# Last cross attention of a decoder kernel: the turn and the projections take other places among the scores, pair 16 is weighed in its own PSUM bank, and GpSimd's last sums wait for a scaling

## What is computed

```python
# self attention: 16 heads of 64, then out projection and residual
z = softmax(q @ k.T / 8) @ v;   x = layernorm(x + (x + z @ w_o))
# cross attention: 2 heads of 64; keys are 154 of the context and the 512 of x itself
ln = layernorm(x) * g + b
q  = ln @ Wq.T
kv = concat([xn_ctx @ Wkv.T, ln @ Wlkv.T]);  k, v = split(kv)
q  = rmsnorm(q, qn_g) / 8;   k = rmsnorm(k, kn_g)
out = softmax(mask(q @ k.T)) @ v @ Wo.T + bo
x  = layernorm(x + out)
```

## Time and profile before

| | |
|---|---|
| median of 3 runs | 696.09 us (694.47 to 698.51) |
| the profiled execution's own time | 697.45 us |
| its span in the profile | 695.7 us |
| PE busy | 617.9 us (89% of the span) |
| DVE busy | 451.1 us (65%) |
| ACT busy | 287.3 us (41%) |
| POOL busy | 246.7 us (35%) |
| mean granted clock of TensorE | 0.951 of full |

### The profile page before, as it was taken

One profiled execution on the slowest core, in us unless ns is written; L12 is line 12 of the kernel. 1 busy time (PEld: TensorE's weight loads), 2 busy tenths in 40 slices (PEclk: granted clock), 3 DMA queues, 4 the chain that ended last, 5 costly groups with the idle time before them and its releaser, 6 DMA issues.

```text
span 695.7 us, 8771 instructions
## 1 busy us (share of the span) xinstructions
PE 617.9 (89%) x3161; PEld 307.6 (44%) x3162; DVE 451.1 (65%) x1172; ACT 287.3 (41%) x548; POOL 246.7 (35%) x178
## 2 busy tenths in 40 slices
PE   8766769998997899999999979997878999999996
PEld 4322457976752322222224422333522446565655
DVE  6999998457679457666765597687626673333234
ACT  7979966032403564444443344341141342212120
POOL 2897443233501554554464444572150100000001
PEclk9957979999998999999999999998997999999999
DMA  8200032030000000000000000001400000000000
GB/s 316 93 0 0 2 121 124 1 122 1 1 1 0 0 1 0 1 0 1 2 0 1 1 0 1 0 1 63 195 0 1 1 1 1 0 1 0 1 1 31
DMA packets 3681, 18.92 MB, mean 27 GB/s; under 512 B 917, under 2 KB 2198, under 8 KB 3126
## 3 DMA queue, kind: packets, MB, share of 16 engines
q1 hardware_dynamic: 3638, 18.36, 6.9%
HBM read 17.84 MB, written 0.52 MB: 26 GB/s over the span
## 4 chain that ended last, share of the span: by engine, by line
PE 62%; DVE 20%; ACT 9%; issue 5%; POOL 4%; POOLq 0%; DVEq 0%; ACTq 0%
PE PS L2339 10%; PE PS L1617 8%; PE PS L2353 6%; DVE SB L1846 6%; PE PS L1562 4%; PE PS L1601 4%; PE PS L1585 3%; PE PS L1687 2%; PE PS L1631 2%; PE PS L2063 2%; DVE SB L199 2%; PE PS L2074 1%; DVE SB L1868 1%; ACT SB L468 1%; POOL SB L238 1%
## 5 line engine op out<-in xcount | busy, mean ns | idle before, releaser
L1832 POOL TENSOR_TENSOR SB<-SB 128x1024 f32<-128x1024 f32 x32 | 75.3, 2353 | 115.3 <-ACT SB L1785 115.3
L1846 DVE TENSOR_REDUCE SB<-PS 128x2 f32<-128x1024 f32 x64 | 78.4, 1225 | 56.7 <-PE PS L1585 56.7
L1785 ACT ACTIVATE SB<-PS 128x1024 f32<-128x1024 f32 x64 | 65.5, 1023 | 101.3 <-PE PS L1604 101.2
L2339 PE MATMUL PS<-SB 128*128 128x512 f32 x176 | 83.1, 609 | 0.2 <-DVE SB L2416 0.2
L1617 PE MATMUL PS<-SB 128*64 128x512 f32 x256 | 69.9, 628 | 1.4 <-DVE SB L1871 1.4
L1601 PE MATMUL PS<-SB 64*128 64x512 f32 x256 | 68.9, 616 | 1.1 <-ACT SB L1789 1.1
L238 POOL TENSOR_TENSOR SB<-SB 128x4 f32<-128x4 f32 x18 | 19.4, 1078 | 133.0 <-DVE SB L204 132.9
L2391 ACT ACTIVATE SB<-PS 128x512 f32<-128x512 f32 (+1 forms) x48 | 28.5, 596 | 90.2 <-PE PS L2339 87.3
L2416 DVE TENSOR_TENSOR SB<-SB,PS 128x512 f32<-128x512 f32 (+1 forms) x48 | 32.6, 686 | 48.1 <-PE PS L2339 43.7
L2353 PEld LDWEIGHTS PS<-SB 128*128 128x128 f32 (+1 forms) x384 | 49.4, 190 | 18.5 <-issue 10.0
L1868 DVE RECIPROCAL SB<-PS 128x512 f32<-128x512 f32 x16 | 53.7, 3355 | 3.9 <-PE PS L1631 3.9
(11 more groups left out here) (401 smaller groups left out, 1132.8 us busy)
## 6 DMA issues: line engine op xcount, KB each, us to landing
SB<-exp SPq DMA_DIRECT2D x1, 4352.0 KB, 14.0
SB<-moe SPq DMA_DIRECT2D x1, 4096.0 KB, 12.3
SB<-dft SPq DMA_DIRECT2D x1, 2304.0 KB, 12.1
SB<-att SPq DMA_DIRECT2D x1, 2048.0 KB, 8.1
SB<-mix SPq DMA_DIRECT2D x1, 768.5 KB, 4.5
SB<-mix SPq DMA_DIRECT2D x1, 640.0 KB, 5.6
SB<-ssm SPq DMA_DIRECT2D x1, 602.0 KB, 6.7
SB<-lat SPq DMA_DIRECT2D x1, 585.0 KB
```

The costliest lines, as they stand in the source:

```text
L1785: act.activation(expd[i % 2][:, 1024 * u:1024 * u + 1024], bank(2 * (u % 2), 2), ACT.Exp).then_inc(sem("d_exp"), 1)
L1832: pool.tensor_tensor(half_sums[half], e[:, 0:1024], e[:, 1024:], ALU.add).then_inc(sem("d_half_sum"), 1)
L1846: dve.tensor_reduce(shift[i % 2][:, qt:qt + DK + 1:DK], two_heads(bank(4, 2)), AX_X, ALU.max, negate=True)\
L2339: pe.matmul(bank(2 * (i % 3) + side), exp_w["e_w13"][:, c:c + 128], xsT[:, 512 * n:512 * n + 512], start=True, stop=True).then_inc(sem(("t ...
```

## The change

Five things, no instruction more or less:

- The weighing of pair 16 goes to bank 0 instead of bank 6 (`heads_bank`), and no longer waits for `d_headed` of pair 15. The out projection of the second batch goes to bank 6 in turn. All four of its steps stand together, with the turn of the context keys and of row tiles 0 and 1 ahead of them, in that order.
- POOL waits for `e_scaled` 3, the scaling of row tiles 2 and 3 on DVE, before the half sums and the sum of pair 16.
- `e_maxima` and the parts of the out projection of batch 2 interleave in another way; the fourth `e_maxima` comes behind the out projection of pair 16, and on DVE its maximum behind the residual and the statistics of the norm.
- In the cross attention the turn of batch 1's normed rows comes ahead of all scores, the projections 4 to 7 come between the first two scores, and the turns of tiles 2 and 3 and the four `e_maxima` of batch 1 come among the scores and weighings of batch 0.
- `shifts(1)` comes ahead of `sums(0)`, and DVE's last sum of batch 0 (`late_sum`, L2264) between its maxima of batch 1.

```diff
     def weigh(i, kt):
             if kt == 0:
                 pe.wait_ge(sem("d_exp"), 4 * i + 4)
-                if i >= 1:
+                if 1 <= i < NP_ - 1:
                     pe.wait_ge(sem("d_headed"), i)
...
-                ins = pe.matmul(bank(6)[head(h), :], v, expd[i % 2][...],
+                ins = pe.matmul(heads_bank(i)[head(h), :], v, expd[i % 2][...],
...
         e_turn_ctx(pe)
-        weigh(last, 0)
-        weigh(last, 1)
+        e_turn_tiles(pe, 0)
+        e_turn_tiles(pe, 1)
+        for kt in range(4):
+            weigh(last, kt)
         e_maxima(pe, 0, 0)
-        weigh(last, 2)
-        weigh(last, 3)
+        pe.wait_ge(sem("d_headed"), last)
+        pe.matmul(bank(6), zeros_low, mask_16[0:1, 0:512], start=True, stop=False)
+        attended_part((0,))
         e_maxima(pe, 0, 1)
         sums(last)
-        pe.matmul(bank(0), zeros_low, mask_16[0:1, 0:512], start=True, stop=False)
-        attended_part((0, 1))
+        attended_part((1, 2))
         e_maxima(pe, 0, 2)
-        attended_part((2, 3))
-        e_maxima(pe, 0, 3)
+        attended_part((3,))
         pe.wait_ge(sem("d_headed"), NP_)
...
         ins.then_inc(sem("d_out"), 1)
+        e_maxima(pe, 0, 3)
...
     def d_pool(pool):
             if i == NP_ - 1:
                 for k in range(3):
                     e_pool_row_norms(pool, k)
+                pool.wait_ge(sem("e_scaled"), 3)
...
     def e_pe(pe):
         shifts(0)
+        turn_half(pe, tiled(xn), "e_normed", 1, 1, 5)
         score(0, 0)
-        for u in range(KT):
...
+        e_project(pe, 4)
+        e_project(pe, 5)
+        score(0, 1)
+        e_project(pe, 6)
+        e_project(pe, 7)
+        weigh(0, 0)
+        score(0, 2)
+        weigh(0, 1)
+        score(0, 3)
         e_turn_tiles(pe, 2)
+        weigh(0, 2)
         e_turn_tiles(pe, 3)
-        for qt in range(4):
-            e_maxima(pe, 1, qt)
+        score(0, 4)
+        weigh(0, 3)
+        e_maxima(pe, 1, 0)
+        score(0, 5)
+        e_maxima(pe, 1, 1)
+        weigh(0, 4)
+        weigh(0, 5)
+        e_maxima(pe, 1, 2)
+        e_maxima(pe, 1, 3)
+        shifts(1)
         sums(0)
-        shifts(1)
         score(1, 0)
...
     def e_dve(dve, follow, headed_of):
         headed_of(NP_ - 1)
         maximum(0, 2)
-        maximum(0, 3)
...
         norm_stats(dve, follow, tiled(xsum), 1)
-        shift_in(0)
+        maximum(0, 3)
         norm_apply(dve, tiled(xsum), tiled(xs), 1).then_inc(sem("stage_done"), 1)
         dve.wait_ge(sem("stage_done"), 4)
         norm_stats(dve, follow, tiled(xs), 1)
+        shift_in(0)
```

More of the change, by code:

```diff
@@ L1565, in d_projection, with heads_bank @@
         return project
+    def heads_bank(i):
+        return bank(6 if i < NP_ - 1 else 0)
     def two_heads(a):
@@ L1735, in d_pe @@
                     e_project(pe, 2 * u + 1)
-                if i == NP_ - 1 and u == 3:
-                    e_turn_tiles(pe, 0)
-                    e_turn_tiles(pe, 1)
                 if before:
@@ L2019, in rough_at @@
     def rough_at(b, qt):
-        return 512 * (1 if b == 0 else 0 if qt % 2 else 5)
+        return 512 * (1 if b == 0 else 0 if qt == 2 else 5)
     def e_maxima(pe, b, qt):
@@ L2032, in e_maxima @@
             pe.wait_ge(sem("d_shift_in"), NP_ + 1)
-        if n == 5:
+        if n == 6:
             pe.wait_ge(sem("d_exp"), 4 * NP_ + KT)
-        if b == 0 and qt or b == 1 and qt >= 2:
-            pe.wait_ge(sem("d_max"), 4 * NP_ + n - b)
+        elif qt:
+            pe.wait_ge(sem("d_max"), 4 * NP_ + n - n // 7)
         at = rough_at(b, qt)
@@ L2051, in shifts @@
             pe.wait_ge(sem("d_max"), 4 * NP_ + 4 * b + 4)
[L2052 removed]
+            pe.transpose(bank((7, 6)[b])[:, 0:128], e_shift[b], ident).then_inc(sem("d_shifts"), 1)
         def score(b, u):
@@ L2080, in sums @@
             if b == 0:
-                pe.wait_ge(sem("d_max"), 4 * NP_ + 7)
+                pe.wait_ge(sem("d_max"), 4 * NP_ + 8)
                 pe.wait_ge(sem("e_first_sum"), 2)
@@ L2149, in turned_rows @@
         def turned_rows(b):
-            act.wait_ge(sem("e_qk_turned"), 2 * b + 1)
+            act.wait_ge(sem("e_qk_turned"), b + 2)
             act.activation(q_T[b], bank((4, 5)[b]), ACT.Copy, scale=q_gain).then_inc(sem("e_qk_T"), 1)
             act.activation(k3[:, b, 256:], bank((5, 7)[b]), ACT.Copy, scale=lat["kn_g"]).then_inc(sem("e_qk_T"), 1)
+        act.wait_ge(sem("e_qk_turned"), 1)
+        act.activation(k3[:, :, 0:256], c4, ACT.Copy, scale=lat["kn_g"]).then_inc(sem("e_qk_T"), 1)
         turned_rows(0)
-        act.wait_ge(sem("e_qk_turned"), 2)
-        act.activation(k3[:, :, 0:256], c4, ACT.Copy, scale=lat["kn_g"]).then_inc(sem("e_qk_T"), 1)
+        e_normed_in(act, 1)
         for b in range(B):
@@ L2162, in e_act @@
                                bias=mask_col[:, 2 * b + u:2 * b + u + 1] if u < 2 else 0.0).then_inc(sem("d_exp"), 1)
+                if b == 0 and u < 2:
+                    e_rows_in(act, 2 * u + 4)
+                    e_rows_in(act, 2 * u + 5)
                 if b == 0 and u == 3:
[L2164 to L2169, removed]
+                    turned_rows(1)
     e_qk = [a.rearrange("p (t w) -> p t w", w=384)[:, :, 0:256] for a in qkv]
@@ L2214, in low @@
         def low(b):
-            dve.wait_ge(sem("e_qk_T"), 3 * b + 1)
+            dve.wait_ge(sem("e_qk_T"), 2 * b + 2)
             dve.tensor_copy(q_16[b], q_T[b]).then_inc(sem("e_qk_16"), 1)
-            dve.wait_ge(sem("e_qk_T"), 3 * b + 2)
+            dve.wait_ge(sem("e_qk_T"), 2 * b + 3)
             dve.tensor_copy(k_16[:, 512 * b:512 * b + 512], k3[:, b, 256:]).then_inc(sem("e_qk_16"), 1)
@@ L2240, in unit_of @@
             follow(dve.reciprocal(e_unit[b], bank(7)))
-        low(0)
-        dve.wait_ge(sem("e_qk_T"), 3)
+        dve.wait_ge(sem("e_qk_T"), 1)
         for h in range(H_C):
             dve.tensor_copy(low_ctx[head(h), :, h, :], k3[head(h), :, 0:S2]).then_inc(sem("e_qk_16"), 1)
+        low(0)
         dve.wait_ge(sem("e_mask"), 3)
@@ L2268, in e_dve @@
         low(1)
-        for qt in range(4):
-            maximum(1, qt)
+        maximum(1, 0)
+        maximum(1, 1)
+        dve.wait_ge(sem("d_exp"), 4 * NP_ + 5)
+        dve.tensor_tensor(late_sum, weights[0][:, 3072:4096], weights[0][:, 4096:5120], ALU.add).then_inc(sem("e_second_sum"), 1)
+        maximum(1, 2)
+        maximum(1, 3)
         shift_in(1)
```

16 lines of the change are left out of this document (6 added, 10 removed).

## The result

The changed kernel takes 699.44 us in the median of 20 runs (696.71 to 702.99); the kernel before, run beside it again, 697.94 us (694.06 to 701.77, 20 runs). The ratio is 1.0034, 95% interval 1.0020 to 1.0047: slower by about 2.4 us, a third of a percent (the two medians lie 1.5 us apart). 698.3 had been forecast from the three runs shown, +2.2 us.

What follows compares the result with a forecast made beforehand. TensorE held 62% of the chain and VectorE 20%, so waits between them counted. Gains up to the normed rows shrink to 0.1 us at the first score; then losses make +2.2 on 696.09: 698.3 us, range 693.2 to 701.8.

Steps and rivals of the forecast that it cites:

- Part 1: From 467 us to the normed rows ending self attention: residual 7.0 us earlier, normed rows 6.6 us earlier.
- the cast beside a sum: VectorE's bf16 casts before the rough maxima: held by GpSimd's sums; maxima at 476.9 us, 475.4 if not held.
- the rival: Casts not held by GpSimd: chain to the normed rows 1.5 us shorter, -1.8 us in all, 696.5 us; chance 0.12.
- The turn ahead of the scores: Start of cross attention: scores wait behind the normed rows' turn, so 6.6 us of gain become 0.1 at the first score.
- GpSimd's order: Cross attention: powers stand behind two sums and the kept residual, so TensorE waits 6.2 us for the row tiles' turn.
- The sum: From 467 us to batch 1's first score: +2.2 us in total, giving 698.3 us on the median.
- the second part: First score of batch 0 to first score of batch 1, which comes at 536.0 us against 533.84.
- The powers do not hold the scaling: Rival in cross attention: powers hold VectorE's scaling, first score of batch 1 +1.5 us, 699.8 us; chance 0.08.
- The low clock lasted: Slower rival: half clock beginning with TensorE's 6 us wait in cross attention lasts 10 us, 700.6 us; chance 0.20.
- The faster rival: Casts before the rough maxima not held by GpSimd: -1.8 us, 696.5 us; chance 0.12.
- its second half: Besides free casts, TensorE leaves its waits at full clock: another -3.3 us, 693.2 us; chance 0.10.

Runs made afterwards that it cites:

- run 2: The changed kernel with GpSimd's last sum of pair 16 behind the four bf16 casts on VectorE; ratio to the kernel before 0.9988.
- run 6: The changed kernel with two scores ahead of the normed rows' turn again and VectorE's first shifts ahead of the second statistics; ratio to the kernel before 1.0013.
- run 1: The changed kernel with GpSimd's two powers for row tiles 4 to 7 ahead of its two first sums; ratio to the kernel before 0.9983.
- run 4: The kernel before with GpSimd's wait for the scaling of row tiles 2 and 3 alone; ratio to the kernel before 0.9947.
- run 9: The changed kernel with edits of run 1, run 2, run 6, batch 0 sums beside the last maximum, first sums awaiting the second scaling; ratio to before 0.9908.
- run 3: The changed kernel without GpSimd's wait for the scaling of row tiles 2 and 3; ratio to the kernel before 1.0029.
- run 11: The kernel before with two GpSimd waits: pair 16's sums behind the scaling, the last of them behind the four casts; ratio 0.9940.

## Why the prediction held

**Part 1.** Scaling 468.3 forecast; counted from the same score it ended 1.0 us behind it there and 1.0 us now (470.23 + 0.76 - 469.99). Maxima forecast 9.6 us behind it, measured 9.3. Residual 20.5, measured 20.4. Normed rows 29.1, measured 28.9. The term that no row of before showed, the cast beside a sum, was taken from the nearest row and was right: run 2 shows what it costs, 2.0 us at the first score against 1.5 in the rival, and 2.2 in the stretch against 1.8.

**The turn ahead of the scores.** First score forecast 30.2, measured 29.9, at half clock (2.08 us). Run 6 bears it out: with the low clock set aside, putting the turn back gives 4.1 us at the first score, of which some 1.7 reach the end while GpSimd's powers are late.

**GpSimd's order.** A wait of 6.2 us was forecast, 6.05 measured; run 1 takes it away, and 4.2 us behind the first score with it, more than the change loses. This was the step that decided.

**The sum.** The stretch was forecast at 68.7 (66.5 + 2.2) and is 67.7. Of the 1.0 us, 0.25 lies ahead of the first score. Most of the rest is a term of the second part that was put too large: the two projections and the second score behind the first score took 2.8 us, not 3.4, for the clock rose at about 502.4 us, right behind the first score. That +1.2 us in the stretch and +2.4 us (1.4 to 3.3) in the times don't agree well. The low clock behind the casts, 1.6 us in three of the five executions with that order but not in the profiled one of the change, may be a part of it; that is not shown.

**The rivals.** The powers do not hold the scaling (0.76 us beside one). The rule of the Trainium skill, "SBUF — State Buffer" (practical consequences), that a VectorE instruction with two SBUF inputs contends with a GpSimd one that reads SBUF is too wide for the powers of 128x8 here; for the sums of 128x1024 the rows agree with it (5.04 us against 0.76). The low clock lasted from about 516 to 522.7 us, not 10 us. The faster rival falls with the casts' 3.03 us, and its second half with the 6.0 us that turn, weighing, turn and score took behind the wait, at half clock.

**What I had wrong**: that one line of the first part carries its gain (run 4), and, in what was expected of run 4, that GpSimd's wait in the kernel before would be worth 1.5 us. I had put the hold of the casts against it and left out that the weighing behind it comes back at full clock (1.94 us instead of 3.67).

## What to carry to other kernels

When a step moves forward on one engine, follow it to the last engine that serves it, and read that engine's order as well: the gain stops at the first queue that did not move. A GpSimd sum beside VectorE's scalings and casts costs whole instructions, so place it by what VectorE does in its 2.4 us, and look at what stands behind what you free. Try the waits one by one: here a single wait in the old order (0.9947) beat the whole change (1.0034), and of two GpSimd waits that each freed a hold, one gained (run 4) and one did not (run 9). Before a distance of one execution is put down to an edit, look whether the same instructions ahead of the edit took the same time.

## What I had not expected of the hardware

The time up to the fourth score of pair 16, before which nothing differs, varies by 5.9 us between the profiled executions of these kernels (465.3 to 471.2 us), with a granted clock of 0.82 in the first 100 us of the kernel before and 0.74 in those of the change. A single time of this kernel says little about a change of 1 to 2 us; the distance between two matmuls that both kernels have says more. But it is not free of the clock either: in one and the same order, behind the same wait of 1.9 us, the clock stayed full in two executions and fell to half in three, which cost 1.6 us.

The same twelve matmuls of the sums took 2.79 us in run 3, 4.22 in the change, 5.02 in run 11 and 5.39 in run 6, at granted clocks of 1.00, 0.65, 0.54 and 0.50. What an edit gains or loses by a wait can be doubled or undone there.
